# Building the edge lists from marks in one stage with the first norm, and a node stage of layer 1 in overlapping steps

## The reference

```python
h = relu(layernorm(x)); x = x + L0(h, edge_weight, src, dst)          # layer 1 of the text below
h = relu(layernorm(x)); x = x + L1(h, edge_index)                     # layer 2
h = relu(layernorm(x)); x = x + L2(h, edge_attr_32, mask, src, dst)   # layer 3
h = relu(layernorm(x)); x = x + L3(h, edge_index, edge_weight, edge_attr_50)
# L0: weighted means over the edges in both directions, then a gated unit
neigh1 = mean(ft[src] * w, by dst); neigh2 = mean(ft[dst] * w, by src)
gi = concat(neigh1 @ W1.T, neigh2 @ W2.T) @ w_ih.T + b_ih;  gh = feat @ w_hh.T + b_hh
r = sigmoid(i_r + h_r); z = sigmoid(i_z + h_z); n = tanh(i_n + r * h_n); out = n + z * (feat - n)
```

## Time and profile before

| what | value |
|---|---|
| median of 3 runs | 10560.45 us (10553.97 to 10576.99) |
| the profiled execution, its own time | 10562.05 us |
| its span, first to last instruction | 10560.1 us |
| mean granted TensorE clock | 0.951 |

### The profile page before, as it was taken

The page is one execution under the profiler, slowest core; times in us unless marked ns, Lnnn a source line. Parts: engine busy times, 40 slices in busy tenths (PEclk is TensorE's granted clock), DMA queues, the critical chain, the costliest instruction groups (busy, mean ns, idle before and its releaser), DMA issues. The chain is left out here.

```text
span 10560.1 us, 239099 instructions
## 1 busy us (share of the span) xinstructions
PE 9122.2 (86%) x62424; PEld 7433.1 (70%) x62425; DVE 5998.2 (57%) x12183; ACT 4706.7 (45%) x11650; POOL 3292.1 (31%) x3487
## 2 busy tenths in 40 slices
PE   0599999999999856999899588898888499999998
PEld 0599999999999824777666356666666366666666
DVE  5666666666666525777511255555555455555555
ACT  0333333333333324444400267777776355555555
POOL 2000000000000000000000067777776177777775
PEclk7799999999999977999899799999999799999999
DMA  2000000000000101222255244444444122222222
GB/s 63 21 3 3 3 3 3 3 3 3 3 3 3 42 2 43 113 113 114 100 192 193 103 117 118 118 118 118 118 118 120 38 72 73 73 73 73 73 73 69
DMA packets 376711, 711.17 MB, mean 67 GB/s; under 512 B 106024, under 2 KB 271838, under 8 KB 356192
## 3 DMA queue, kind: packets, MB, share of 16 engines
q0 software_dynamic: 136544, 335.76, 11.5%
q1 hardware_dynamic: 239744, 368.85, 10.0%
HBM read 552.51 MB, written 151.69 MB: 67 GB/s over the span
## 5 line engine op out<-in xcount | busy, mean ns | idle before, releaser
L1537 POOL DMA_INDIRECT x<-table,p_gidx x1632 | 1543.2, 946 | 2483.9 <-ACT p_gidx L1574 2024.4
L2038 POOL DMA_INDIRECT c_G<-table,c_gidx x1632 | 1551.7, 951 | 505.3 <-issue 492.0
L708 PE MATMUL g_ps_cell<-g_kw,g_loh 128*128 128x98 f32 x9472 | 1237.5, 275 | 161.1 <-issue 86.9
L708 PEld LDWEIGHTS g_ps_cell<-g_kw,g_loh 128*128 128x128 f32 x9472 | 1162.9, 194 | 170.1 <-issue 94.8
L683 ACT COPY g_AT<-g_ps_turn 128x384 f32<-128x384 f32 (+1 forms) x1258 | 578.7, 466 | 1503.5 <-PE g_ps_turn L738 1503.5
L718 PE MATMUL g_ps_slot<-h,g_A 128*128 128x129 f32 x7252 | 1049.2, 282 | 0.0
L593 POOL DMA_INDIRECT g_hrow<-table,dst_tab x74 | 69.8, 944 | 3135.7 <-PE g_ps_rev L729 3135.2
L1628 PE MATMUL p_ps_sum<-x 128*96 128x256 f32 x3264 | 890.9, 397 | 173.6 <-DVE hid L1563 158.1
L729 PE MATMUL g_ps_rev<-g_hrow,g_AT 128*128 128x129 f32 x7252 | 1024.4, 279 | 0.5 <-ACT g_AT L683 0.5
L623 DVE TENSOR_TENSOR x<-x,g_ps_rev 128x387 f32<-128x387 f32 (+1 forms) x1258 | 671.1, 538 | 605.2 <-PE g_ps_rev L729 605.2
L729 PEld LDWEIGHTS g_ps_rev<-g_hrow,g_AT 128*128 128x128 f32 x7252 | 923.4, 196 | 1.8 <-ACT g_AT L683 0.7
(11 more groups left out here) (348 smaller groups left out, 15400.5 us busy)
## 6 DMA issues: line engine op xcount, KB each, us to landing
adj_save<-a_A SPq DMA_DIRECT2D x74, 1568.0 KB, 5.1
a_A<-adj_save SPq DMA_DIRECT2D x74, 1568.0 KB, 6.6
c_ed<-in_edge_dram SPq DMA_DIRECT2D x1632, 25.0 KB
x<-table,p_gidx POOLq DMA_INDIRECT x1632
p_lhs<-in_edge_dram SPq DMA_DIRECT2D x1632, 16.0 KB
c_G<-table,c_gidx POOLq DMA_INDIRECT x1632
x<-in_x_dram SPq DMA_DIRECT2D x2, 3328.0 KB, 13.6
table<-m_rows SPq DMA_DIRECT2D x17, 384.0 KB, 2.5
```

The lines of the kernel that those rows point to most:

```text
L708: last = pe.matmul(ps_cell[q % 2][:, r * KEYS:(r + 1) * KEYS], loh[:, b, cell, :], kw[:, b, cell, :], start=True, stop=True)
L1537: g.indirect_dma_start(G[:, H * b + q, :], None, table2, bass.IndirectOffsetOnAxis(ap=gidx[:, b, q:q + 1], axis=0)).then_inc(gathered[b], 16)
L2038: g.indirect_dma_start(G[:, H * b + q, :], None, table, bass.IndirectOffsetOnAxis(ap=gidx[:, b, q:q + 1], axis=0)).then_inc(gathered[b], 16)
```

## The change

Four things are done.

1. `stage_tables`, `stage_cells` and the first `stage_norm` become one `stage_lists`. The first node of each edge tile is loaded once, 13 values a partition (`tile_firsts`, 13 = TK). VectorE works out at which cell and at which pair each tile starts, and splits that number into a group (of 37) and a place in it (of 128). Two one-hot tables of these (128x962 and 128x3328, BF16) are multiplied on TensorE (26 instructions), which leaves a mark where a tile starts; a scan of 128 columns and a product with a triangle of ones give the tile of each cell and pair. All 50 gathers then fetch rows of `edge_ends` in groups of 4 tiles (LP) through a ring of 6 buffers. While they run VectorE makes the norm's statistics and ScalarE the 52 activations; then the groups are turned, cells first and pairs behind them. h is stored in four parts.
2. The reverse sums are read where they lie. `rev_save` and its two stores and 13 loads are gone; x comes in by steps into a double buffer.
3. `stage_gru_nodes` is unrolled with double buffers and more semaphores: TensorE turns step c + 1 before the gates of step c and turns the update of step c - 1 back behind them. The inverse weights of all tiles are made once. The `bn_stats` for the next norm are made here (`measure`).
4. `stage_gcn_out` is unrolled with two buffers and makes the `bn_stats` for layer 3; `stage_norm` leaves them out there and in layer 2 (`measured`), and is unrolled.

The core of the diff:

```diff
-LP = 8
+LP = 4
+RING = 6
-    rev_save = dram("rev_save", (P, NT, D + 1))
...
+        def stage_lists(h, key_tab, lo_tab, w_tab, rel_tab, dst_tab, cnt_tab, first_row):
...
+                        for k in range(CT):
+                            at = slice(k * NCH, (k + 1) * NCH)
+                            sp.wait_ge(normed, (k + 1) * NCH)
+                            sp.dma_start(tiles(table)[:, at, :], h[:, at, 0:D]).then_inc(stored, 16)
+                        sp.wait_ge(taken, LG + PG)
                         sp.dma_start(edge_save, edge_tab[:, :, :]).then_inc(saved, 16)
...
+                        g.wait_ge(tiles_known, 1)
+                        for k, (which, g0, m) in enumerate(groups):
+                            if k >= RING:
+                                g.wait_ge(turned, before[k - RING + 1])
+                            for j in range(m):
+                                at = which * LG + g0 + j
+                                g.indirect_dma_start(ends[:, k % RING, j, :, :].rearrange("p k e -> p (k e)"), None, a["edge_ends"],
+                                                     bass.IndirectOffsetOnAxis(ap=tix_i[:, at:at + 1], axis=0)).then_inc(ends_in[k % RING], 16)
...
+                        for k, (oh, w) in enumerate(((ohg, LG), (ohr, P))):
+                            v.tensor_tensor(oh[:, :, :, :].rearrange("p l t c -> p (l t) c"),
+                                            part[:, k, :, :].rearrange("p l t -> p (l t)").unsqueeze(2).to_broadcast([P, 2 * TK, w]),
+                                            numbers[:, 0:w].unsqueeze(1).to_broadcast([P, 2 * TK, w]), ALU.is_equal).then_inc(oh_made, 1)
+                        v.wait_ge(marks_made, 1)
+                        then(v.tensor_copy(marks[:, :, :].rearrange("g l c -> g (l c)"), ps_marks[0:LG, 0:2 * P]))
+                        for k in range(2):
+                            v.tensor_tensor_scan(incl[:, k, :], one[:, :], marks[:, k, :], 0.0, ALU.mult, ALU.add).then_inc(incl_made, 1)
+                        v.wait_ge(offs_made, 1)
...
+                        v.wait_ge(list_turned, 1)
+                        v.tensor_copy(tix_i[:, :], ps_list[:, 0:2 * LG]).then_inc(tiles_known, 1)
...
+                        v.wait_ge(x_in, 16)
+                        for t in range(NT):
+                            v.bn_stats(stat[:, t, :], x[:, t, :]).then_inc(stats_in, 1)
+                        v.wait_ge(stats_in, NT)
+                        merge_stats(v, 0, merged)
+                        invert_std(v, std_in, scaled)
+                        for k, (which, g0, m) in enumerate(groups):
+                            e, b = ends[:, k % RING, 0:m, :, :], k % 2
+                            key_g, low_g = key[:, b, 0:m, :], low[:, b, 0:m, :]
+                            v.wait_ge(*ends_seen(k))
+                            if k >= 2:
+                                v.wait_ge(turned, before[k - 1])
+                            if which == 1:
+                                v.tensor_copy(key_g, e[:, :, 0, :])
+                                for j in range(m):
+                                    last = v.tensor_scalar(low[:, b, j, :], e[:, j, 1, :], start[:, LG + g0 + j:LG + g0 + j + 1], None, ALU.subtract)
+                                last.then_inc(keys_made, 1)
+                                continue
...
+                        pe.wait_ge(oh_made, 2)
+                        for k in range(2):
+                            for t in range(TK):
+                                last = pe.matmul(ps_marks[0:LG, k * P:(k + 1) * P], ohg[:, k, t, :], ohr[:, k, t, :], start=t == 0, stop=t == TK - 1)
+                        last.then_inc(marks_made, 1)
+                        pe.wait_ge(consts, 9)
+                        pe.wait_ge(incl_made, 2)
...
+                        for k, (which, g0, m) in enumerate(groups):
+                            pe.wait_ge(keys_made, k + 1)
+                            for j in range(m):
+                                at = before[k] + j
+                                if at >= 4:
+                                    pe.wait_ge(taken, at - 3)
...
+                        for t in range(NT):
+                            s.activation(h[:, t, 0:D], x[:, t, :], ACT.Relu, bias=nmr[:, t:t + 1], scale=rstd[:, t:t + 1]).then_inc(normed, 1)
...
+                                    s.copy(edge_tab[:, :, cols], pt[at % 4][:, 0:3 * P].rearrange("p (k t) -> p k t", k=3)).then_inc(taken, 1)
...
+                    if not measured:
+                        for t in range(NT):
+                            v.bn_stats(stat[:, t, :], x[:, t, :]).then_inc(stats_in, 1)
+                        v.wait_ge(stats_in, NT)
+                    merge_stats(v, 0, merged)
+                    invert_std(v, std_in, scaled)
...
-                    @block.sync
-                    def _(sp):
-                        sp.wait_ge(rev_added, TGS * NBATCH + 2)
-                        sp.dma_start(rev_save[:, 0:NT - 1, :], rev[:, :, :]).then_inc(saved, 16)
-                        sp.dma_start(rev_save[:, NT - 1:NT, :], rev[:, NT - 2:NT - 1, :]).then_inc(saved, 16)
...
+                        def turn(c):
+                            pe.wait_ge(means_ready, 2 * c + 2)
+                            if c >= 1:
+                                pe.wait_ge(fm_ready, c)
+                            for k in range(3):
+                                for t in range(count(c)):
...
+                        def make_gates(c):
+                            pe.wait_ge(fm_ready, c + 1)
+                            for g in range(2):
+                                if c >= 1:
+                                    pe.wait_ge(rz_ready, 2 * (c - 1) + g + 1)
...
-                        with pe.Fori(0, NCH) as c:
-                            pe.wait_ge(*V.now("h", c))
-                            pe.wait_ge(*S.before("fm", c))
...
+                        turn(0)
+                        for c in range(NCH + 1):
+                            if c + 1 < NCH:
+                                turn(c + 1)
+                            if c < NCH:
+                                make_gates(c)
+                            if c >= 1:
+                                turn_back(c - 1)
...
+                        def means(c):
+                            if c >= 2:
+                                v.wait_ge(turned, c - 1)
+                            for k, rows in enumerate((fwd, rev)):
+                                v.tensor_tensor(nodes[:, c % 2, k, 0:count(c), :], rows[:, tiles_in(c), 0:D],
+                                                inv[:, k, tiles_in(c)].unsqueeze(2).to_broadcast([P, count(c), D]), ALU.mult).then_inc(means_ready, 1)
...
+                        def add(c):
+                            v.wait_ge(turned_back, c + 1)
+                            v.wait_ge(x_in[c % 2], 16 * (c // 2 + 1))
+                            v.tensor_tensor(x[:, tiles_in(c), :].rearrange("p t d -> p (t d)"), xin[:, c % 2, 0:count(c), :].rearrange("p t d -> p (t d)"),
+                                            ps_back[:, 0:cols(c)], ALU.add).then_inc(added, 1)
+                        def measure(c):
+                            v.wait_ge(added, c + 1)
+                            for t in range(CT * c, CT * c + count(c)):
+                                v.bn_stats(stat[:, t, :], x[:, t, :]).then_inc(stats_in, 1)
...
-                        v.wait_ge(x_in, 16)
-                        with v.Fori(0, NCH) as c:
-                            rev = tot[:, bass.ds(c, 1), :, :].rearrange("p o t d -> p (o t) d")
-                            v.wait_ge(rev_in, 16 * (c + 1))
...
+                        means(0)
+                        for c in range(NCH + 2):
+                            if c + 1 < NCH:
+                                means(c + 1)
+                            if c < NCH:
+                                candidate(c)
+                            if c < NCH:
+                                update(c)
+                            if 1 <= c <= NCH:
+                                add(c - 1)
+                            if c >= 2:
+                                measure(c - 2)
+                        v.wait_ge(rest_in, 16)
+                        for t in range(NTQ, NT):
+                            v.bn_stats(stat[:, t, :], x[:, t, :]).then_inc(stats_in, 1)
...
+                        take(0)
+                        for c in range(NCH):
+                            if c + 1 < NCH:
+                                take(c + 1)
+                            gate(c)
+                            squash(c)
...
+                        def add(c):
+                            v.wait_ge(turned, c + 1)
+                            now = x[:, CT * c:CT * (c + 1), :].rearrange("p t d -> p (t d)")
+                            v.tensor_tensor(now, now, ps_back[c % 2][:, :], ALU.add).then_inc(added, 1)
+                        def measure(c):
```

(25 more changed lines are left out.)

689 lines of the change are left out of this document (307 added, 382 removed).

## The result

The changed kernel takes 10161.76 us in the median of 4 runs (10154.51 to 10170.82), the kernel before 10557.21 us (10553.84 to 10576.99) beside it: a ratio of 0.962, with a 95% interval of 0.9605 to 0.9639. So 395 us are saved, where 436.5 were forecast; the predicted 10124 us is 38 us too low and within its range. The profiled execution took 10154.51 us, with a span of 10152.8; that of before 10562.05, with a span of 10560.1.

A forecast was written before the change was run, and what follows sets the result against it. Outside TensorE-bound sums, engines wait on one another in the list and node stages. Savings 270.8 + 8.9 (reverse sums) + 120.3 + 15.5 + 21.1 + 2.9 - 3 = 436.5 us, from 10562.05, gave a median of 10124 us; range 10090 to 10195.

The forecast's parts named there:

- The lists: List stage ahead of layer 1's sums: 388.8 us would fall to 118, saving 270.8 before 3 us for contention.
- First gather: List stage: GpSimd's first gather would start 19 us into the span, with 15 to 27 as bounds.
- statistics: List stage: VectorE's 52 statistics for the first norm, at 0.24 us each, would take 12.6 us.
- stall: List stage: the fourth cell group would wait 4 us, as ScalarE, busy with activations, frees TensorE's PSUM buffers late.
- the contention: List stage: gathers beside VectorE work would slow about 90 one-source instructions, +3 us taken, bounds 0 and +24.
- rival 3: List stage: VectorE and GpSimd hold each other, 0.27 us an instruction or 0.94 a gather; +24 us, 10145 us; chance 0.12.
- The node stage: Layer 1 node stage: 363.9 us would fall to 243.7 with steps of 18.4 us, saving 120.3.
- the chain: Node stage: from gates' end through candidate, update, add, statistics and means to the next turn, 6.85 us a step.
- The gates: Node stage: TensorE's gate products would take 9.0 us a step, with bounds 8.0 and 16.0.
- Rivals 2 and 4: Node stage: TensorE stays at 1.2 GHz, 10201 us, chance 0.10 (2); stays at 2.4 GHz, 10099 us, 0.08 (4).
- The norms: Norms and last convolution stage: savings of 15.5 us in layer 2, 21.1 in layer 3, 2.9 in layer 4.
- rival 5: Layer 1 sums stage: TensorE loses clock, 0.86 in place of 0.98, making the kernel slower than before; chance 0.01.

## Why the prediction was near, and where it was wrong

**The lists: right, 8 us too little.** First gather 17.1 for 19, statistics 10.1 for 12.6, stall 3.8 for 4, sums at 112.9 for 118, or 121 with the contention. The gathers stay hidden. The contention is there, a gather here taking 1025 ns in the mean (51.3 us for 50) against the 946 before, and it lies with GpSimd, where it costs nothing: beside the statistics the gathers take 946 ns as before, beside the key work up to 1451. VectorE loses almost nothing. A group of four tiles took 6.56 us with five gathers beside it and 6.48 with three. The one subtraction in such a group that is longer than the others takes 357 ns for 277, and the most that any instruction of the groups took over its like is 0.17 us (592 ns for 420, once). So rival 3 falls, since VectorE is not held by 0.27 us an instruction nor by a whole gather. The Trainium skill (SBUF — State Buffer, Who interferes with whom) describes a lock for a whole instruction. On VectorE's side the trace does not show it; the three gathers that took 1.38 to 1.45 us, some 0.5 more than the rest, lay beside VectorE instructions of 0.69 us, so on GpSimd's side the trace has holds, if shorter than the whole of such an instruction.

**The node stage: the chain right, two terms too dear.** The gates were taken at 9.0 us and took 8.2, the chain at 6.85 and took 6.25, so a step took 17.1 to 18.0 us for the 18.4 forecast; the first gates ended 25.8 us in, for 31.3, and the end behind the last full gates (3660.93 to 3671.05) took 10.1 for 12.0. Together 20.5 us. Rivals 2 and 4 fall, since the two rows of the clock differ: over a step the granted clock was 0.80, in the gates alone 0.97, in the turns alone 0.50. The turns, behind a wait of 5.9 us, run at 1.2 GHz, and the gates behind them at 2.4.

**The norms: right in size**, the last convolution stage 4 and layer 4 3 us cheaper than forecast, by the same faster row of statistics.

**The sums: the step that failed.** The prediction took this stage as untouched: "The change leaves the instructions of the former alone", and, in rival 5, "Nothing in its streams changed but its surroundings". It gave 0.01 to the stage losing time, and only by the clock. It lost 56.7 us, by two things that hang together: the head of a loop of 1638 instructions stood at another place, because the code ahead of it had another length, and behind each pause for loading the products passed at the lower clock. It is also what the prediction had named as a sign of being wrong, a stage taken as untouched moving by over 10 us. The row that could have warned was on the page of before: 86.9 us of "issue", and the list of waits has them as 34 pauses, one for each return to the loop's head. I had read this page for shares and not asked what the pause was. It was no rounding error: in the sums stage, taking the pauses away is worth 198 us of the changed kernel and 141 of the kernel before, as much as the whole node stage brought.

**The rest: 8 us slower, not settled.** Such stages differ between runs by that much. The stage of layer 3's nodes with the norm behind it, the same code in both, took 231.4 us at a granted clock of 0.80 with the head of the sums loop at place 0, and 247.1 at 0.75 with it at 32; that difference is more than the 8 us by which the latter run stands above its neighbours. What sets the clock there is open.

So the total was near because the errors have opposite signs: some 36 us of savings not seen, against 57 + 8 us of losses not seen. That leaves 29 us in the profiled executions (436.5 - 407.3); the other 9 of the 38 are that the changed kernel's profiled execution is 7.3 us below its median, where that of before was taken as 1.6 above. That they partly cancel is luck. With the head at place 168, where the sums stage has the one pause of the kernel before, the changed kernel took 10085.57 us in its one run: 38 us below the forecast and just outside its range.

## What to carry to other kernels

A pause of an engine that waits for nothing, once for each turn of a loop, was here the loading of instructions: count the pauses against the turns, and look at the packets of the instruction queue. Take the loop's length from the trace and not from the program. Where the loop is loaded anew, the code ahead of it is part of its price, and a change that adds or removes instructions ahead of it on that engine can move it, here by 0.7 to 2% of the kernel's time; fix the place of a long loop's head, or announce its branch, before you compare two versions. And in a pipeline written out by hand, look for the operation that the next step needs and that stands in a queue behind this step's chain: moved two steps ahead, 1.3 us of work a step took 7.6 us off each step, 5.9 of them the wait and most of the rest the higher clock behind it.

## What the runs showed of the hardware that was not expected

- TensorE's loop of 1638 instructions, 6.4 blocks of 256, was loaded anew in each turn (9.0 blocks of 16 KB) or not at all, by the place of its head: places 0, 32, 64 and 104 of 256 (the end at 1742 at most) not at all, 168 (1806), and 20 short of the end, in each turn. 96 instructions more at place 104 (1838) brought the loads back.
- The block of the head started to come 1.0 us behind the branch back, and took 1.0 us in the median of the changed kernel, 1.7 in that of the kernel before.
- A pause of 2.2 to 2.8 us cost 4.2 us a turn, and two pauses of together 3.5 us cost 5.8, since products behind them ran at 1.2 GHz (eight in 1.93 us for 1.06).
- One instruction that announces the branch was worth as much as the right place (9955.52 and 9950.85 us).
- Gathers on GpSimd took 946 ns beside VectorE's statistics and up to 1451 beside its 0.69 us instructions; VectorE's own took 0.08 us more now and then, 0.17 at most.
- 52 statistics in one row take 10.14 us, 0.195 each; in a loop they took 15.5.
